# Row maxima spread over a pair's slots, normalisation moved to ScalarE and small batch arithmetic to GpSimd, in a transformer layer with routed experts

## The reference, cut to what matters

```python
q = einsum('bld,dhk->blhk', x, Wq)                  # 16 heads of 64
latent = einsum('bld,dc->blc', x, Wkv_down)         # 64 wide, shared by all heads
k, v = latent @ Wk_up, latent @ Wv_up
attn = softmax(where(causal, q k^T / 8, -inf))
x1 = layernorm(x + (attn v) @ Wout)
probs = softmax(x1 @ w_router)                      # 32 experts, 8192 tokens
top1, gate = argmax(probs), max(probs)
pos = number of earlier tokens of the same expert   # kept where pos < C = 320
slot = top1 * C + pos
y = (silu(buf @ w_gate) * (buf @ w_up)) @ w_down    # buf: the tokens, by slot
out = layernorm(x1 + gate * y)                      # x1 alone where not kept
```

## Time and profile before

| what | value |
|---|---|
| time, median of 3 runs | 2511.35 us (2507.96 to 2512.93) |
| the profiled execution | 2510.11 us, span 2508.0 us |
| TensorE matmul busy | 2345.6 us, 94% |
| VectorE busy | 1602.7 us, 64% |
| ScalarE busy | 1015.1 us, 40% |
| GpSimd busy | 1678.9 us, 67% |
| granted TensorE clock, mean | 0.967 |

### The profile page before, as it was taken

The page is one execution under the profiler, slowest core; times in us unless marked ns, Lnnn a source line. Parts: engine busy times, 40 slices in busy tenths (PEclk is TensorE's granted clock), DMA queues, the critical chain, the costliest instruction groups (busy, mean ns, idle before and its releaser), DMA issues.

```text
span 2508.0 us, 36804 instructions
## 1 busy us (share of the span) xinstructions
PE 2345.6 (94%) x11528; PEld 1517.6 (61%) x11528; DVE 1602.7 (64%) x4618; ACT 1015.1 (40%) x1992; POOL 1678.9 (67%) x1623
## 2 busy tenths in 40 slices
PE   6999999999999999999999999999999999949996
PEld 4555575556655665566555665566556655537774
DVE  4677657765676667765776567666776577335553
ACT  3445424443444334542444334433444344212222
POOL 1688756975787757875797568766787579623444
PEclk8999999999999999999999999999999999969998
DMA  3222100200011001100020001100110001224652
GB/s 87 60 64 81 39 14 14 73 18 14 18 49 37 18 10 39 47 18 13 18 69 18 14 18 51 35 18 9 43 43 18 18 14 55 68 79 155 193 180 68
DMA packets 96818, 118.96 MB, mean 47 GB/s; under 512 B 12289, under 2 KB 75783, under 8 KB 96625
## 3 DMA queue, kind: packets, MB, share of 16 engines
q1 hardware_dynamic: 89712, 99.98, 14.5%
q0 software_dynamic: 6912, 16.64, 1.9%
HBM read 46.91 MB, written 37.90 MB: 34 GB/s over the span
## 4 chain that ended last, share of the span: by engine, by line
PE 76%; DVE 13%; issue 6%; POOL 1%; ACT 1%; DMA 0%; DVEq 0%; SPq 0%; POOLq 0%; ACTq 0%
PE value_ps L722 18%; PE misc_ps L744 9%; PE turned_ps L699 9%; PE turned_ps L702 8%; PE misc_ps L621 8%; PE turned_ps L891 6%; PE row_ps L674 6%; PE turned_ps L674 3%; PE misc_ps L734 3%; DVE masked_row L1117 2%; DVE q_hl L1098 2%; DVE q_hl L1097 2%; DVE rinv L1151 1%; PE misc_ps L770 1%; DVE x L1199 1%
## 5 line engine op out<-in xcount | busy, mean ns | idle before, releaser
L964 ACT ACTIVATE probs<-turned_ps 128x512 f32<-128x512 f32 (+2 forms) x1280 | 652.1, 554 | 815.2 <-PE turned_ps L702 801.2
L504 POOL TENSOR_TENSOR half_sums<-half_sums,probs 128x1024 f32<-128x1024 f32 (+3 forms) x512 | 832.4, 1626 | 33.2 <-ACT probs L964 15.9
L722 PE MATMUL value_ps<-probs,lat_keys 128*64 128x512 f32 (+3 forms) x3072 | 597.7, 511 | 0.0
L699 PE MATMUL turned_ps<-q_hl,lat_hi 128*128 128x512 f32 (+2 forms) x1280 | 529.7, 414 | 1.5 <-ACT fold_v L1009 1.5
L702 PE MATMUL turned_ps<-q_max,lat_lo 65*128 65x512 f32 (+2 forms) x1280 | 483.7, 378 | 2.5 <-DMA q_max<-both_rows 2.5
L479 POOL TENSOR_SCALAR_AFFINE_SELECT probs<-probs 128x256 f32<-128x256 f32 x512 | 210.3, 411 | 405.0 <-ACT probs L964 404.1
L1117 DVE CUSTOM_DVE_ANT_0 masked_row<-row_ps,future 128x512 bf16<-128x512 f32 (+4 forms) x707 | 347.3, 511 | 189.6 <-PE row_ps L674 184.2
L499 POOL TENSOR_TENSOR half_sums<-probs 128x768 f32<-128x768 f32 (+1 forms) x128 | 269.4, 2105 | 140.8 <-ACT probs L964 118.2
L674 PE MATMUL row_ps<-lat_hi,q_hl 128*128 128x512 f32 (+4 forms) x1026 | 324.3, 356 | 33.0 <-DVE neg_max L1117 18.5
L722 PEld LDWEIGHTS value_ps<-probs,lat_keys 128*64 128x64 f32 x3072 | 190.5, 139 | 265.3 <-issue 199.8
L699 PEld LDWEIGHTS turned_ps<-q_hl,lat_hi 128*128 128x128 f32 x1280 | 244.6, 191 | 137.3 <-issue 107.9
(11 more groups left out here) (191 smaller groups left out, 2652.3 us busy)
## 6 DMA issues: line engine op xcount, KB each, us to landing
q_max<-q_hl SPq DMA_DIRECT2D x256, 128.0 KB
slots_x<-router SPq DMA_DIRECT2D x8, 1290.0 KB, 6.0
ex_x<-slots_x SPq DMA_DIRECT2D x64, 129.0 KB, 2.4
x_in<-in_L_attn_x_bld SPq DMA_DIRECT2D x8, 1024.0 KB, 5.5
layer_out<-x_in SPq DMA_DIRECT2D x8, 1024.0 KB, 4.5
ex_w<-in_L_ffn_w_gate SPq DMA_DIRECT2D x32, 256.0 KB, 3.7
ex_w<-in_L_ffn_w_up SPq DMA_DIRECT2D x32, 256.0 KB, 3.8
ex_w<-in_L_ffn_w_down SPq DMA_DIRECT2D x32, 256.0 KB, 4.3
```

What stands on the lines that cost most here:

```text
L504: nc.gpsimd.tensor_tensor(total, total, now[:, :, q0:BANK], ALU.add).then_inc(added, 1)
L699: nc.tensor.matmul(scores_of(n, h), lat_hi[b % 2][:, keys], q_hl[gp % 2][:, heads, cols], start=True, stop=False)
L722: mm = nc.tensor.matmul(value_ps[h * LD:(h + 1) * LD, q0:BANK], lat_keys[b % 2][:, j, :], probs[:, n % NPROBS, h, q0:BANK], start=(j == 0) ...
L964: nc.scalar.activation(probs[:, n % NPROBS, heads, q0:BANK], scores_of(n, h), ACT.Exp).then_inc(exp_done, 1)
```

## The change

The 24 units of the next pair are given to twelve *places* in place of the twelve slots. A place is (slot, 0), behind the scores and ahead of the values, as before, or (slot, 1), at the end of the slot, behind the values and the slot's other stages. VectorE takes them in the same order. From batch 1 on, the normalisation of x1 becomes eight activations on ScalarE (`normalise_tile`) with a shift that GpSimd makes; the last batch keeps it on VectorE (L1199 of before). `destinations` goes to GpSimd, into p4 slot 3, and so do the add into the earlier counts (L1242 of before), the two small operations behind the variance (L1194) and those of the experts' normalisation. `roots` stands one slot earlier, the sends one pair later (p5 and p6), and TensorE's `count` also waits for the earlier counts. `var_ready` now comes from the last aggregation. The line numbers of the changed kernel are higher; L717, L742, L745 and L765 are L674, L699, L702 and L722 of before.

```diff
-    UNITS_AT = {(gp, t): [(gp + 1, u) for u in range(2 * t, 2 * t + 2)] for gp in range(PAIRS - 1) for t in range(NSLOT)}
+    PLACES = [(0, 0), (0, 1), (1, 1), (2, 1), (4, 0), (4, 1), (6, 0), (7, 0), (8, 0), (8, 1), (10, 0), (10, 1)]
+    UNITS_AT = {(gp, *place): [(gp + 1, 2 * k), (gp + 1, 2 * k + 1)]
+                for gp in range(PAIRS - 1) for k, place in enumerate(PLACES)}
     for t in range(HPB):
-        UNITS_AT[0, t] = [(0, u) for u in range(2 * HPB + 4 * t, 2 * HPB + 4 * t + 4)] + UNITS_AT[0, t]
+        UNITS_AT[0, t, 0] = [(0, u) for u in range(2 * HPB + 4 * t, 2 * HPB + 4 * t + 4)] + UNITS_AT.get((0, t, 0), [])
...
+    NORMALISE_AT = [(1, 9), (1, 10), (1, 11), (2, 0), (2, 4), (2, 5), (2, 6), (2, 6)]
...
                 pool.wait_ge(var_ready, b * 2 + hf + 1)
+                nc.gpsimd.tensor_scalar(var_eps[:, tiles], mean_var[:, tiles, 1], EPS, None, ALU.add).then_inc(eps_added, 1)
+                nc.gpsimd.tensor_scalar(rt[:, 9, tiles], mean_var[:, tiles, 0], -1.0, None, ALU.mult).then_inc(eps_added, 1)
+                pool.wait_ge(eps_added, 2 * (b * 2 + hf + 1))
                 nc.gpsimd.tensor_tensor(rstd[:, tiles], var_eps[:, tiles], minus_half[:, tiles], ALU.pow
                                         ).then_inc(rstd_ready, 1)
                 pool.wait_ge(rstd_ready, b * 2 + hf + 1)
+                nc.gpsimd.tensor_tensor(rt[:, 6, tiles], rt[:, 9, tiles], rstd[:, tiles], ALU.mult).then_inc(x1_shift_ready, 1)
...
+            def destinations(b):
+
+                pool.wait_ge(counted, b + 1)
+                nc.gpsimd.tensor_scalar(rt[:, 5, :], rt[:, 3, :], float(C), None, ALU.mult).then_inc(route_step, 1)
+                nc.gpsimd.tensor_scalar(rt[:, 7, :], rt[:, 4, :], float(C), FAR, ALU.is_ge, ALU.mult).then_inc(route_step, 1)
+                pool.wait_ge(route_step, 6 * b + 1)
+                nc.gpsimd.tensor_tensor(rt[:, 5, :], rt[:, 5, :], rt[:, 4, :], ALU.add).then_inc(route_step, 1)
+                pool.wait_ge(route_step, 6 * b + 3)
+                nc.gpsimd.tensor_tensor(rt[:, 8, :], rt[:, 5, :], rt[:, 7, :], ALU.add).then_inc(route_step, 1)
...
+                nc.gpsimd.tensor_scalar(x1[:, :, GATE], rt[:, 2, :], 0.5, None, ALU.mult).then_inc(route_step, 1)
+                nc.gpsimd.tensor_copy(x1[:, :, TOKEN].bitcast(I32), token_f[:, :]).then_inc(route_step, 1)
+                pool.wait_ge(route_step, 6 * (b + 1))
+                nc.gpsimd.tensor_scalar(token_f[:, :], token_f[:, :], float(L), None, ALU.add).then_inc(routed, 1)
+                nc.gpsimd.tensor_scalar(send_idx[:, :], rt[:, 8, :], float(SLOTS), None, ALU.add).then_inc(send_ready, 1)
+                if b < LAST:
+                    nc.gpsimd.tensor_tensor(earlier[:, :, :], earlier[:, :, :],
...
-                    if b and (p, t) in ((1, 8), (2, 2)):
+                    if b and (p, t) in ((1, 7), (2, 1)):
                         roots(b - 1, p - 1)
-                    if b and p in (4, 5) and t < HPB:
-                        send(b - 1, (p - 4) * HPB + t)
+                    if b and (p, t) == (4, 3):
+                        destinations(b - 1)
+                    if b and p in (5, 6) and t < HPB:
+                        send(b - 1, (p - 5) * HPB + t)
...
                     for use in LATE[gp, t]:
                         STAGES[use[0]](*use[1:])
+                    for unit in UNITS_AT.get((gp, t, 1), []):
+                        row_scores(*unit)
...
+            def normalise_tile(b, i):
+
+                act.wait_ge(x1_shift_ready, b * 2 + i // HPB + 1)
+                ins = nc.scalar.activation(x1[:, i, 0:D], x1[:, i, 0:D], ACT.Identity,
+                                           bias=rt[:, 6, i:i + 1], scale=rstd[:, i:i + 1])
...
-                    if b and (p, t) == (3, 11):
-                        destinations(b - 1)
                     if b and (p, t) in ((1, 5), (2, 0)):
                         variance(b - 1, p - 1)
-                    if b and (p, t) in ((1, 10), (2, 4)):
-                        normalise(b - 1, p - 1)
+                    for unit in UNITS_AT.get((gp, t, 1), []):
+                        row_max(*unit)
```

More of the change, by code:

```diff
@@ L116, in build_layer @@
         lat_keys = [sb(f"lat_keys{i}", [P, NT, LD], F32, attn) for i in range(2)]
+        q_hl = [sb(f"q_hl{i}", [P, 2, L], F32R, attn) for i in range(2)]
         fold_v = sb("fold_v", [P, NPAIR, D], F32, attn)
-        q_hl = [sb(f"q_hl{i}", [P, 2, L], F32R, attn) for i in range(2)]
         q_max = sb("q_max", [LD + 1, 2, 2, BANK], F32R, attn)
@@ L219, in build_layer @@
         rstd_ready = sem("rstd_ready")
+        eps_added = sem("eps_added")
+        x1_shift_ready = sem("x1_shift_ready")
+        counted = sem("counted")
+        earlier_ready = sem("earlier_ready")
+        route_step = sem("route_step")
         x1_ready = sem("x1_ready")
@@ L284, in build_layer @@
             if b and p == 2:
-                for use, t in zip([(hf, kd) for hf in range(2) for kd in range(KD)], (3, 5, 7, 10)):
+                for use, t in zip([(hf, kd) for hf in range(2) for kd in range(KD)],
+                                  (3, 5, 7, 10)):
                     late[t].append(("x1T", b - 1, *use))
@@ L404, in load_weights @@
                 for m, w in enumerate((w_gate, w_up, w_down)):
-                    sp.dma_start(ex_w[k][:, m], w[e].rearrange("(k p) f -> p k f", p=P)).then_inc(ex_loaded[k], 16)
+                    sp.dma_start(ex_w[k][:, m], w[e].rearrange("(k p) f -> p k f", p=P)
+                                 ).then_inc(ex_loaded[k], 16)
             def load_rows(e):
@@ L561, in _ @@
                 roots(LAST, hf)
+            destinations(LAST)
             for i in range(NT):
@@ L571, in root @@
                 pool.wait_ge(var_ready, 2 * B + g + 1)
+                nc.gpsimd.tensor_scalar(neg_mean[:, part], mean_var[:, part, 0], -1.0, None, ALU.mult).then_inc(eps_added, 1)
+                nc.gpsimd.tensor_scalar(var_eps[:, part], mean_var[:, part, 1], EPS / 4, None, ALU.add).then_inc(eps_added, 1)
+                pool.wait_ge(eps_added, 2 * (2 * B + g + 1))
                 nc.gpsimd.tensor_tensor(rstd[:, part], var_eps[:, part], minus_half[:, part], ALU.pow
@@ L777, in count @@
                 pe.wait_ge(onehot_ready, b + 1)
+                if b:
+                    pe.wait_ge(earlier_ready, b)
                 nc.tensor.matmul(bank[:, 0:NT * E], before_bf[:, :], onehot[:, :, :].rearrange("p t e -> p (t e)"),
@@ L849, in _ @@
                         STAGES[use[0]](*use[1:])
-                    for unit in UNITS_AT.get((gp, t), []):
+                    for unit in UNITS_AT.get((gp, t, 0), []):
                         row_scores(*unit)
@@ L1022, in _ @@
                             STAGES[use[0]](*use[1:])
+                    for i, at in enumerate(NORMALISE_AT):
+                        if b and (p, t) == at:
+                            normalise_tile(b - 1, i)
                     if b and p == 3 and t < NT:
@@ L1187, in variance @@
             def variance(b, hf):
-                tiles = slice(hf * HPB, (hf + 1) * HPB)
                 settle()
@@ L1191, in variance, with normalise @@
                     last = nc.vector.bn_aggr(mean_var[:, i, :], stat6[:, i, :])
-                step(last)
-                settle()
-                nc.vector.tensor_scalar(var_eps[:, tiles], mean_var[:, tiles, 1], EPS, None, ALU.add).then_inc(var_ready, 1)
-            def normalise(b, hf):
-                dve.wait_ge(rstd_ready, b * 2 + hf + 1)
-                for i in range(hf * HPB, (hf + 1) * HPB):
+                last.then_inc(var_ready, 1)
+            def normalise(b, tiles):
+                for i in tiles:
+                    dve.wait_ge(rstd_ready, b * 2 + i // HPB + 1)
                     last = nc.vector.tensor_scalar(x1[:, i, 0:D], x1[:, i, 0:D], mean_var[:, i, 0:1], rstd[:, i:i + 1],
                                                    ALU.subtract, ALU.mult)
-                last.then_inc(x1_ready, 1)
+                    if i % HPB == HPB - 1:
+                        last.then_inc(x1_ready, 1)
             over = lambda k: rt[:, k, :].unsqueeze(2).to_broadcast([P, NT, E])
@@ L1241, in count_tiles @@
                 settle()
[L1242 to L1257 removed]
+                nc.vector.reciprocal(rt[:, 2, :], rt[:, 1, :]).then_inc(counted, 1)
             STAGES = {"xT": low_x, "lat": low_latents, "keys": copy_keys, "q": low_q, "maxT": copy_max, "sums": invert,
@@ L1321, in _ @@
                 if use[0] == "rest" and use[2] == NT - 1:
-                    normalise(LAST, 0)
+                    normalise(LAST, range(HPB))
                     variance(LAST, 1)
-                    normalise(LAST, 1)
+                    normalise(LAST, range(HPB, NT))
             def copy_rows(e):
@@ L1360, in add_to_rows @@
                     last = nc.vector.bn_aggr(mean_var[:, g % 2 * NY + n, :], stat6[:, g % 2 * NY + n, :])
-                step(last)
-                settle()
```

(4 more changed lines are left out.)

21 lines of the change are left out of this document (6 added, 15 removed).

## The result

| | before | changed |
|---|---|---|
| median of runs, us (4 each) | 2509.65 (2506.58 to 2512.93) | 2442.29 (2441.89 to 2442.65) |
| ratio | | 0.9731, 95% interval 0.9714 to 0.9748 |
| profiled execution, us (span) | 2510.11 (2508.0) | 2441.89 (2440.1) |
| mean granted clock | 0.967 | 0.974 |

The account below looks back on a forecast made before the run. TensorE, its matmuls covering 94% of the span, bounds the kernel; its idle 6% and low clock can be won. Waits of 50.9 us plus 15.8 of clock, less 1.4, give 65.3 off 2510.1: 2445 us, range 2422 to 2476.

Parts of the forecast that it names:

- units spread: Units issued earlier: 0.44 us won at t = 4 in 39 pairs (17.2), 0.45 at t = 3 in 21 (9.5).
- waits and low clock of p2, p3, p4: Waits won: 12.5 us in p2, 8.9 in p3, 2.8 in p4; low clock won: 15.8 us.
- last pair, tail and experts: End of attention, second half's roots and last pair of experts: a loss of 1.4 us, bounds 0.5 to 8.
- Rival C: The small waits only move to a new meeting point on VectorE: 26.7 us fall away, 2472 us; chance 0.18.
- At t = 8 "nothing": Plain pairs, unit 17 waiting for unit 14: nothing changes ahead of unit 14, so no gain; upper bound 8 us.
- Normalisation: p2, t = 6: the 2.13 us wait becomes one of 0.35 once ScalarE normalises; 7 x 1.78 = 12.5 us.
- Counting and addresses: p3, t = 11: 0.25 of 1.52 us stays, 8.9 won; p4, t = 1: 1.40 goes in two batches, 2.8 won.
- I cost it at nothing: GpSimd's added 3.5 us a batch and later sends delay nobody, covered by 4.6 us idle a pair; cost nothing.
- rival E: GpSimd becomes the bound if its new small operations cost 1.035 us each: 2553 us; chance 0.05.
- Clock: Low clock in every p4 (12.4 us) and one stretch of a p2 (3.4) goes with the waits: 15.8 us won.
- rival B: The waits go but the clock falls as often, somewhere else: 2461 us; chance 0.22.
- rival D: Waits at t = 8 also go (8 us), clock holds after the logits in half the batches (about 8): 2429 us; chance 0.08.

Follow-up runs that it names:

- run 1: The changed kernel with the units back to two per slot, the engine moves kept: 2471.9 us (0.9849).
- run 8: The changed kernel with VectorE's first half of the row inversions at slot 7 instead of slot 6: 2435.5 us (0.9710).
- run 6: The kernel before with only GpSimd's roots one slot earlier (slots 7 and 1 instead of 8 and 2): 2483.1 us (0.9898).
- run 3: The changed kernel with only the normalisation back on VectorE at its old slots: 2437.6 us (0.9719).
- run 4: The changed kernel with the address arithmetic and the add into the earlier counts back on VectorE: 2463.2 us (0.9822).
- run 10: The changed kernel with 20 more small dependent GpSimd instructions at slot 0 of p5 in 7 batches, their results unread: 2491.6 us (0.9931).
- run 11: The changed kernel with 50 more small dependent GpSimd instructions at slot 0 of p5 in 7 batches, their results unread: 2559.5 us (1.0203).
- run 2: The kernel before with the units in their twelve new places and no move between engines: 2491.7 us (0.9927).

## Why the prediction was right, step by step

The sum was 65.3 us and the spans differ by 67.9. Its parts, from the pair lengths of the two traces (they add to 67.8):

| part | forecast | measured |
|---|---|---|
| units spread (plain pairs, t = 3) | 26.7 | 26.3 |
| waits and low clock of p2, p3, p4 | 24.2 + 15.8 = 40.0 | 47.9 |
| last pair, tail and experts | -1.4 | -4.1 |
| setup | 0 | -2.3 |

- **Units spread: right.** 0.43 a plain pair against 0.44 (bounds 0 and 0.49), and 0.67 became 0.20 at t = 3. Against run 1, where the other moves are in already, spreading is worth 29.6 us. Rival C is out. At t = 8 "nothing" was right too; run 8 later found 6.8 us there, with another edit.
- **Normalisation: the number right, its cause wrong.** "Four normalisations hold VectorE for 3.86 us" took a duration for work. Of the 3.86, 2.5 was standstill beside GpSimd, since four take 1.36 where it leaves them alone; the shortest in the same trace is 0.40, and the step should have asked why the mean in the loop is twice that. The changed kernel holds two edits that bear on this wait, and the prediction weighed one. The roots, moved by one slot, are enough: runs 6 and 3 lose the wait with the normalisation still on VectorE. The move to ScalarE with the roots left late was not run; it would, I take it, clear VectorE of this work as well, but it was not needed. With the roots early it is a small loss, since the new wait, forecast at 0.35, is there in each batch (timeline of TensorE in the changed kernel),

```profile
389.03 0.63 PE L805 MATMUL misc_ps<-ident,x 128*128 128x128 f32 x4 [0.39 <-ACT x L1024]
```

7 x 0.39 = 2.7 us, and with the longest, 0.55 in batch 7, 2.9 in all. The other 1.8 of the 4.7 us between the two kernels is about the start of the first pair, 53.2 against 51.3, which no run ties to the change. The prediction's 0.41 for one activation was the distance between two in a row, not its length: 3.28 us for eight holds eight of 0.49 that overlap. The normalising one, which has a shift besides the scale, is 0.60 long, and two in a row take 1.09.
- **Counting and addresses: undersized.** I left 0.25 of p3's 1.52; the wait at its end is gone in all seven batches, and 0.1 us of idle time is left in a p3 in the mean. Undoing it alone costs 20.9 us (run 4). There p3 and p4 are 1.66 and 1.95 us longer, 25.2 us in seven batches: 7 x 1.79 and 2 x 1.77 = 16.1 of waits, and half of 17.1 us more at the low clock, 8.5. Against that, its first pair starts 2.2 us earlier, and p2 is 0.13 shorter. The step had 11.7 and no clock of its own.
- **GpSimd: "I cost it at nothing, what covers that is 4.6 us a pair" was wrong by a factor of three.** In the pair that carries the sends, 1.5 us are covered (runs 10, 11). "Nothing" held all the same in batches 1 to 6, since p4, rid of its sends, has 2.1 us to spare (24.88 busy of 27.00) and p5 1.6. Where p6 is short, in the last batch, GpSimd did not "recover in p6": two waits of 1.10 and 1.06 us and 0.6 more at the heads make up the 2.7 that the tail's term lacks. GpSimd's small instructions cost 199 to 266 ns, as taken, so rival E fails on its price; had they cost 1.035 us, runs 10 and 11, which loaded p5, suggest that what went beyond the idle time would indeed have been paid.
- **Clock: the total low, and the price of p4's share not what it seemed.** The low clock fell from 71.7 to 27.3 us. Where it stands tells more than the sum:

| us at 1.2 GHz | middle of p2 | end of p2, start of p3 | end of p3, p4 |
|---|---|---|---|
| before | 10.2 | 37.5 | 23.9 |
| changed | 0 | 27.3 | 0 |
| run 2 | 20.5 | 41.0 | 20.5 |
| run 4 | 0 | 23.9 | 20.5 |
| run 6 | 0 | 13.7 | 13.7 |
| the other runs | 0 | 20.5 to 30.7 | 0 |

In the middle of p2 the clock falls only in the two kernels where TensorE waits 1.97 or 2.46 us at slot 6 there, and at the end of p3 and in p4 only in the four where it waits 1.5 to 1.8 us for the counting and the addresses. So rival B is out: those falls did not turn up elsewhere. At the end of p2 or the start of p3 it falls in every kernel, in the changed one in six of seven batches, so rival D is out too; half of the 10.2 us less there, 5.1, stood in no term. The rule quoted from the Trainium skill, that long waits for a DMA are what costs the clock, would have given zero; these rows speak against it as the only cause, since the waits here were for VectorE. But a wait does not always bring a fall: in run 6 all seven p3 end in a wait of 1.5 us, and the clock falls behind four of them. And a fall at the start of p4 cost nothing of its own. Two p4 of run 6, without a fall and with one:

```profile
438.12:467.60 29.48, 27.47 (x135) 16.28 (x134) 23.03 (x66) 13.20 (x26) 25.49 (x24) 1.00 0.21 66
1770.78:1800.26 29.48, 28.88 (x135) 16.71 (x134) 23.02 (x66) 13.23 (x26) 25.36 (x24) 0.94 0.21 66
```

Both take 29.48 us. At the full clock TensorE comes early to slot 1 and waits 1.4 there for VectorE; at the low clock it comes late and does not wait. Only a fall that comes behind that wait adds to it (31.05 and 30.98 us in batches 3 and 4 of run 6). In the kernel before five of the seven falls in p4 are of the first kind. Of the 12.4 us that the prediction booked to p4's clock, these five, 8.9 by an estimate of 1.77 each, would by these rows have come back as waits had the clock alone been mended. They were won because the address arithmetic left VectorE, which takes away wait and fall together: p4 as a whole went from 29.79 to 26.99, 7 x 2.80 = 19.6 us.

## What to carry to other kernels

Before work is moved off a busy engine, compare each instruction's duration at the suspect place with the shortest of the same form in the trace: if it is several times that, look at what the neighbour engine runs in the same microsecond, since moving the neighbour by one slot may take the wait away (here 24.8 us for one line) and moving the work may not be needed. An engine's room for more work was here its idle time in the fullest stretch, not in the mean one; loading it on purpose measures it. The low clock and a wait on another engine can hide each other, so that their prices may not be added without a kernel that has one without the other. And a prediction that is right in total still wants its terms tested one by one: here one of 12.5 us had the right number and the wrong cause.
